# A fused AdaLN block on one core: value rows of two key groups projected token by feature, with the convolution's shift done by a DMA

## What is computed

```
h = layernorm(x) * (1 + ca) + sa                  # modulation rows from silu(c) @ wmod
qkv = h @ W_pack                                  # 16 query heads, 8 key and value groups, 128 wide
q, k = rope(q), rope(k)
k = conv_k[0] * k[token - 1] + conv_k[1] * k      # per group; token -1 counts as zero
v = conv_v[0] * v[token - 1] + conv_v[1] * v
attn = softmax(mask(q k^T / sqrt(128))) v         # causal, window of 128 tokens
x = x + ga * (attn @ W_o)
h = layernorm(x) * (1 + cb) + sb
x = x + gb * moe(h)                               # 32 experts, top 4, capacity 128, and a shared expert
```

## Time and profile before

| | |
|---|---|
| median of 3 runs | 765.53 us (765.27 to 766.3) |
| profiled execution | 769.37 us, of it 766.9 span from first to last instruction |
| mean granted TensorE clock | 0.99 of full speed |
| busy share of the span | PE 95%, PEld 81%, DVE 69%, ACT 61%, POOL 55% |
| chain that ended last | PE 76%, DVE 11%, ACT 6%, DMA 2% |
| share of that chain on the projections (L1335 into PJ) | 22% |

### The profile page before, as it was taken

One profiled execution on the slowest core, in us unless ns is written; L12 is line 12 of the kernel. 1 busy time (PEld: TensorE's weight loads), 2 busy tenths in 40 slices (PEclk: granted clock), 3 DMA queues, 4 the chain that ended last, 5 costly groups with the idle time before them and its releaser, 6 DMA issues.

```text
span 766.9 us, 12813 instructions
## 1 busy us (share of the span) xinstructions
PE 731.1 (95%) x4114; PEld 620.8 (81%) x4114; DVE 531.6 (69%) x1552; ACT 467.7 (61%) x1277; POOL 425.5 (55%) x337
## 2 busy tenths in 40 slices
PE   3899999999999999999999999999988999999997
PEld 3688889998899898889989888989866767777775
DVE  4598788679877768987776797778665215564373
ACT  5688878777886677788667777877554212222110
POOL 0644445554466488646647875654534517468356
PEclk9999999999999999999999999999999999999999
DMA  8960005800005011100401101040359689996772
GB/s 294 322 136 1 2 1 175 287 1 2 1 1 168 26 40 48 40 1 1 158 8 40 46 28 62 16 165 1 123 145 237 191 289 272 282 240 74 163 233 82
DMA packets 62353, 84.42 MB, mean 110 GB/s; under 512 B 6312, under 2 KB 50229, under 8 KB 62288
## 3 DMA queue, kind: packets, MB, share of 16 engines
q1 hardware_dynamic: 51440, 70.56, 29.8%
q0 software_dynamic: 7680, 8.95, 6.2%
q10 hardware_dynamic: 3168, 4.11, 1.5%
HBM read 54.81 MB, written 33.51 MB: 115 GB/s over the span
## 4 chain that ended last, share of the span: by engine, by line
PE 76%; DVE 11%; ACT 6%; DMA 2%; issue 2%; POOL 1%; SPq 0%; ACTq 0%; POOLq 0%
PE PJ L1335 22%; PE OUT L1443 9%; PE U L1428 6%; PE U L1388 6%; PE U L1593 5%; PE U L1417 4%; PE U L1387 3%; PE U L1429 3%; PE U L1335 3%; PE OUT L1539 3%; PE U L1539 2%; PE XB L1612 2%; PE OUT L1612 2%; PE XB L1335 2%; ACT U L546 1%
## 5 line engine op out<-in xcount | busy, mean ns | idle before, releaser
L768 POOL TENSOR_TENSOR qsw<-qsw,sinT 128x512 f32<-128x512 f32 x96 | 126.2, 1314 | 184.6 <-ACT qsw L533 183.7
L977 DVE CUSTOM_DVE_ANT_0 U<-U,mask 128x128 f32<-128x128 f32 (+1 forms) x256 | 86.6, 379 | 54.8 <-PE U L1388 54.4
L546 ACT ACTIVATE U<-U,nmax 128x128 f32<-128x128 f32 (+1 forms) x256 | 100.4, 392 | 32.2 <-DVE nmax L977 31.7
L1335 PE MATMUL PJ<-hT_hi,w_hi 128*128 128x512 f32 x256 | 113.8, 445 | 4.0 <-DVE hT_lo L951 3.7
L1335 PE MATMUL PJ<-hT_lo,w_hi 128*128 128x512 f32 x256 | 103.5, 404 | 0.0
L1335 PE MATMUL PJ<-hT_hi,w_lo 128*128 128x512 f32 x256 | 103.1, 403 | 0.0
L772 POOL TENSOR_TENSOR qr<-qr,qsw 128x512 f32<-128x512 f32 x64 | 82.5, 1289 | 31.3 <-DVE qr L965 30.8
L532 ACT ACTIVATE qsw<-PJ 64x512 f32<-64x512 f32 x96 | 57.0, 594 | 58.1 <-PE PJ L1335 49.3
L779 POOL DMA_INDIRECT slot_rows<-xn,sidx x64 | 64.4, 1006 | 45.6 <-issue 12.0
L1443 PE MATMUL OUT<-wo_hi,oT_hi 128*128 128x256 f32 x256 | 83.0, 324 | 1.4 <-DVE wo_lo L1001 1.2
L994 DVE TENSOR_TENSOR oT_lo<-U,oT_hi 128x256 fp32r<-128x256 f32 x128 | 54.1, 423 | 41.2 <-ACT oT_hi L553 41.0
(11 more groups left out here) (212 smaller groups left out, 1827.6 us busy)
## 6 DMA issues: line engine op xcount, KB each, us to landing
wgu<-in_dram SPq DMA_DIRECT2D x32, 352.0 KB, 9.4
expert_sum<-blank SPq DMA_DIRECT2D x3, 2176.0 KB, 17.8
slot_rows<-blank SPq DMA_DIRECT2D x1, 4624.0 KB, 26.3
late_sums<-expert_sum SPq DMA_DIRECT2D x9, 512.0 KB, 8.9
wd_a<-in_dram SPq DMA_DIRECT2D x12, 352.0 KB
wraw<-in_dram SPq DMA_DIRECT2D x8, 512.0 KB, 11.5
bcm<-mod_rows SPq DMA_DIRECT2D x8, 512.0 KB, 6.8
xe<-slot_rows ACTq DMA_DIRECT2D x10, 289.0 KB, 6.3
```

The lines of the kernel that those rows point to most:

```text
L546: last = act.activation(U[n % 3][:, a:z], U[n % 3][:, a:z], ACT.Exp, scale=-1.0, bias=nmax[:, n % 4, j:j + 1], accum_out=rsum[:, n % 4, j: ...
L768: pool.tensor_tensor(pair3(qsw[:, n % NQSW, :]), pair3(qsw[:, n % NQSW, :]), both(sinT[:, :]), ALU.mult).then_inc(t2_done, 1)
L977: last = dve.tensor_tensor_reduce(out=U[n % 3][:, a:z], in0=U[n % 3][:, a:z], in1=allowed, scale=-float(HD) ** -0.5, scalar=3.4e38, op0=AL ...
L1335: last = pe.matmul(out_ap, a(c), b_(c), start=(n == 0), stop=(n == len(steps) - 1))
```

## The change

The values are projected the other way round: the tokens of `hT` are the weights and 256 columns of `w_pack`, two value groups, are the moving side. One value turn makes one sequence of two groups, two blocks of 128 tokens by 256 features in one bank, with 12 matmuls of 256 columns. There are still 32 value turns, listed with the others in `TURNS`: each group of four units has one (group 0 has two, the last none), so the turns run one ahead and LEAD becomes 5. The order in which the projection weights are prepared (`W_ORDER`) changes with it.

The tokens now lie on partitions, and the shift by a token is a shift by a partition. ACT scales the bank by the first tap, one activation per group, into a `qsw` slot (which value turns now share with q and k; slots go by turn number). `next_token` on ACT then issues two DMAs, from SBUF to SBUF: rows 0 to 126 of both blocks to partitions 1 to 127 of `vsh`, and the last row of block 0 to partition 0 of block 1. DVE multiplies the bank by the second tap into `vN`, and POOL adds `vsh` (`earlier_token`, one step after the evacuation, behind the rope of that step). `v_transpose`, `v_rows`, `vT` and `v0` are gone. A `qsw` slot is reused three turns later, after the rope of that turn, or after the DMAs if it was a value turn. `XB` is ordered by the hooks' own semaphores, and `yg` shares memory with `xnT_lo`, with one more wait in `post_gate`.

```diff
-LEAD = 4
-W_ORDER = (4, 0, 6, 1, 5, 2, 7, 3)
+LEAD = 5
+W_ORDER = (4, 0, 6, 1, 7, 5, 2, 3)
+TURNS = []
+for _G in range(NU // 4):
+    TURNS += [("k", _G, 0), ("q", _G, 0)]
+    TURNS += [("v", v, 0) for v in ((0, 1) if _G == 0 else (_G + 1,)) if v < NV]
+    TURNS += [("q", _G, 1)]
...
 @block.scalar
+            def project(u):
+                kind, i, _ = TURNS[u]
+                bank, slot = PJ[u % 2], u % NQSW
+                act.wait_ge(pj_ps, u + 1)
+                if u >= NQSW:
+                    if TURNS[u - NQSW][0] == "v":
+                        v = TURNS[u - NQSW][1]
+                        act.wait_ge(ld_vsh[v % 2], 32 * (v // 2 + 1))
+                    else:
+                        act.wait_ge(rope_done, rope_number(u - NQSW) + 1)
+                if kind == "v":
+                    for g in range(2):
...
+                        last = act.activation(qsw[:, slot, :].rearrange("p (t c) -> p t c", t=2)[:, :, heads],
+                                              bank[:, :].rearrange("p (t c) -> p t c", t=2)[:, :, heads], ACT.Copy,
+                                              scale=cwv[:, tap:tap + 1])
+                    last.then_inc(pj_act, 1)
                     return
...
+            def next_token(u):
+                v = TURNS[u][1]
+                rows_v = qsw[:, u % NQSW, :].rearrange("p (t c) -> p t c", t=2)
+                act.wait_ge(pj_act, u + 1)
+                if v >= 2:
+                    act.wait_ge(v_done, v - 1)
+                act.dma_start(vsh[1:PN, v % 2, :, :], rows_v[0:PN - 1, :, :]).then_inc(ld_vsh[v % 2], 16)
+                act.dma_start(vsh[0:1, v % 2, 1, :], rows_v[PN - 1:PN, 0, :]).then_inc(ld_vsh[v % 2], 16)
...
             for n in STEPS:
-                if 0 <= n - 1 < NU and n % 4 == 1:
-                    v_rows(n // 4)
-                if 0 <= n + 3 < NU:
-                    project(n + 3)
+                if 0 <= n + LEAD - 1 < NU:
+                    project(n + LEAD - 1)
                 if 0 <= n - 2 < NU:
                     head_high(n - 2)
+                if 0 <= n + LEAD - 1 < NU and TURNS[n + LEAD - 1][0] == "v":
+                    next_token(n + LEAD - 1)
                 if 0 <= n < NU:
                     exps_of(n)
...
 @block.gpsimd
+            def earlier_token(u):
+                if TURNS[u][0] != "v":
+                    return
+                v = TURNS[u][1]
+                pool.wait_ge(ld_vsh[v % 2], 32 * (v // 2 + 1))
+                pool.wait_ge(pj_dve, u + 1)
+                pool.tensor_tensor(v_tile(v), v_tile(v), vsh[:, v % 2, :, :], ALU.add).then_inc(v_done, 1)
...
             for n in STEPS:
-                if 0 <= n + 3 < NU:
-                    rope(n + 3)
+                if 0 <= n + LEAD - 1 < NU:
+                    rope(n + LEAD - 1)
+                if 0 <= n + LEAD - 2 < NU:
+                    earlier_token(n + LEAD - 2)
...
 @block.vector
+                    dve.tensor_tensor(v_tile(i).rearrange("p t (g d) -> p t g d", g=2),
+                                      PJ[u % 2][:, :].rearrange("p (t g d) -> p t g d", t=2, g=2), tap,
+                                      ALU.mult).then_inc(pj_dve, 1)
...
 @block.tensor
+                if kind == "v":
+                    for t in range(2):
+                        tk = slice(i % 2 * S + t * PN, i % 2 * S + (t + 1) * PN)
+                        last = halves(PJ[u % 2][:, t * 2 * HD:(t + 1) * 2 * HD], HC,
+                                      ((lambda c: hT_hi[:, p % 2, c, tk], lambda c: hT_lo[:, p % 2, c, tk]), weights))
...
-            def v_transpose(G):
...
-                    if n % 4 == 0:
-                        v_transpose(n // 4)
```

More of the change, by code:

```diff
@@ L251, in adaln_block @@
             sem(n) for n in ("var1", "rstd1_done", "xhat_done", "ht_ps", "ht_used", "h_hi_done", "h_lo_done"))
-        pj_ps, pj_act, pj_dve, t2_done, rope_done, k0_done, kc_done, vt_ps, vn_done = (
-            sem(n) for n in ("pj_ps", "pj_act", "pj_dve", "t2_done", "rope_done", "k0_done", "kc_done", "vt_ps", "vn_done"))
+        pj_ps, pj_act, pj_dve, t2_done, rope_done, k0_done, kc_done, v_done = (
+            sem(n) for n in ("pj_ps", "pj_act", "pj_dve", "t2_done", "rope_done", "k0_done", "kc_done", "v_done"))
         sc_ps, sneg_done, exp_done, rinv_done, norm_done, pt_ps, pt_done, pv_ps, ot_done = (
@@ L298, in adaln_block, with columns, w_chunks @@
         WO_PART = NH // len(WO_STEPS)
[L300 to L305, removed]
+        def columns(u):
+            kind, i, h = TURNS[u]
+            g = i % GROUPS
+            first = {"k": (NH + g) * HD, "q": (2 * g + h) * HD, "v": (NH + NKV) * HD + (g // 2) * 2 * HD}[kind]
+            j, at = divmod(first, WC)
+            return j, slice(at, at + (2 * HD if kind == "v" else HD))
+        def w_chunks(u):
+            return W_ORDER.index(columns(u)[0]) + 1
         def x_pair(p):
@@ L317, in pair3, with rope_number, rope_buffer, v_tile @@
             return ap.rearrange("p (b s) -> p b s", b=2)
[L319 to L324, removed]
+        def rope_number(u):
+            return sum(kind != "v" for kind, _, _ in TURNS[:u])
+        def rope_buffer(u):
+            kind, G, h = TURNS[u]
+            return kr[:, :] if kind == "k" else qr[:, h, G % 2, :]
+        def v_tile(v):
+            return vN[:, v // 2 % 2, v % 2, :, :]
         def later(n):
@@ L527, in project @@
                     return
-                rope = rope_number(m)
-                if rope >= NQSW:
-                    act.wait_ge(rope_done, rope - NQSW + 1)
                 half = HD // 2
-                act.activation(qsw[0:half, rope % NQSW, :], bank[half:HD, :], ACT.Copy)
-                act.activation(qsw[half:HD, rope % NQSW, :], bank[0:half, :], ACT.Copy).then_inc(pj_act, 1)
+                act.activation(qsw[0:half, slot, :], bank[half:HD, :], ACT.Copy)
+                act.activation(qsw[half:HD, slot, :], bank[0:half, :], ACT.Copy).then_inc(pj_act, 1)
@@ L1202, in _ @@
                     head_low(n - 2)
-                if n % 4 == 3 and n + 1 < NU:
+                if n % 4 == 3 and 0 <= n + 1 < NU:
                     k_conv((n + 1) // 4)
-                if 0 <= n + 3 < NU:
-                    project(n + 3)
+                if 0 <= n + LEAD - 1 < NU:
+                    project(n + LEAD - 1)
                 if 0 <= n < NU:
@@ L1422, in weighted_v @@
                 pe.wait_ge(pt_done, n + 1)
-                if n % 4 == 0:
-                    pe.wait_ge(vn_done, G + 1)
+                if G % 2 == 0 and n % 4 < 2:
+                    pe.wait_ge(v_done, G + b + 1)
                 o = U[n % 3][:, 0:S]
-                v = vN[:, G % 2, b * S:(b + 1) * S]
-                pe.matmul(o, v[:, 0:PN], pT[:, n % 2, 0:S], start=True, stop=False)
-                pe.matmul(o[:, PN:S], v[:, PN:S], pT[:, n % 2, S:S + PN], start=False, stop=True).then_inc(pv_ps, 1)
+                v = vN[:, G // 2 % 2, b, :, G % 2 * HD:(G % 2 + 1) * HD]
+                pe.matmul(o, v[:, 0, :], pT[:, n % 2, 0:S], start=True, stop=False)
+                pe.matmul(o[:, PN:S], v[:, 1, :], pT[:, n % 2, S:S + PN], start=False, stop=True).then_inc(pv_ps, 1)
             def output(n):
```

139 lines of the change are left out of this document (59 added, 80 removed).

## The result

The changed kernel takes 954.99 us (median of 4 runs, 949.93 to 956.37) beside 765.4 us (762.47 to 766.3) for the kernel before: 1.2465 times as long, 95% interval 1.2427 to 1.2504. The forecast was 855 us with a range of 798 to 945: the direction came out and the mechanism in part, the size did not, and the time lies outside the range. The profiled execution took 956.4 us with a span of 954.5, against 769.4 and 766.9 before: +187.6 us of span.

What follows compares the result with a forecast made beforehand. TensorE bounds the kernel before; the one-engine copy's loop was to replace it. Loop groups and extras +69 us, start +21, prologue and tail -1, together +89 on 765.5: 855 us, range 798 to 945.

Steps and rivals of the forecast that it cites:

- The loop: Per group: issue, landing, addition, k's rotation, k tap, value evacuation, next issue, 17.8 us, replacing TensorE as bound.
- the landing: The 127-row copy to vsh, on one DMA engine, lands after 11.9 us; bounds 10.7 to 12.6.
- the sum: Loop groups with extras +69 us, start +21, prologue and tail -1: +89 on the 765.5 us median, 855 us.
- landings under traffic: Copies landing late: 10 us beside the zeroing of the sums; 4 us for the pairs' own loads.
- scatters behind the addition, ACT's hooks, routing: Extras above the loop: scatters before k's rotation 7 us, hooks before value evacuation 7, three pair-routing groups 7.
- the start: First two copies, issued near 26 and 29 us under traffic, land near 45 and 56; +21 us.
- the tail: One projection fewer at the end, 1.48 us partly hidden; together with the longer prologue -1 us.
- the issues: ACT's two DMA issues take some 0.7 us while oT_hi is copied; exponentials behind wait for DVE's k convolution anyway.
- The cheap parts: Value projection +0.03 us a group, 1 us in all; ACT about even; POOL's addition 1.29 us a group.
- the first rival: Copy spread over the engines lands in 2.5 us, TensorE stays the bound: about -5, 760.5 us; chance 0.11.
- The third, "halfway": One engine slower alone, near 1070 us; halfway, landing 14.5, loop 20.4, +180, 945 us; chance of slower than 945: 0.05.
- the signs named for the forecast: Addition waits 5 to 6 us; score matmuls 17 to 19 apart, waiting for q's rotation or kc; TensorE about 85%.

Runs made afterwards that it cites:

- e8: The changed kernel with a separate qsw slot for values and POOL's addition one iteration later, behind the next k's rotation; 918.8 us.
- e2: The changed kernel with its two DMAs swapped, the single row issued first and the 127-row copy behind it; 938.5 us.
- e4: The changed kernel with the 127-row copy cut into 79 rows (one engine) and 48 rows (16 engines), plus the single row; 821.4 us.
- e6: The changed kernel without the shift's DMA copies and without POOL's addition; 751.0 us, 0.9835 of the kernel before.
- e7: The changed kernel without the shift's DMA copies but with POOL's addition (of zeros) kept in place; 763.1 us, 0.9989 of the kernel before.
- e1: The changed kernel with the 127-row copy cut into 112 and 15 rows, plus the single row; 787.2 us, 1.0256 times the kernel before.
- e12: e1's copies, addition behind the next k's rotation, issues behind the exponentials, then SyncE's in a new program order from the fourth value turn; 763.3 us.

## Why the forecast had the right direction and the wrong size

**The loop was a right step, but not the only bound.** A group of the kernel after without scatters or bulk traffic (a quiet one), in which the single row's issue passed in 0.56 us (timeline, POOL and ACT; idle time and releaser in brackets):

```profile
462.12 0.63 ACTq L563 DMA_DIRECT2D vsh<-qsw  x1
462.79 0.56 ACTq L564 DMA_DIRECT2D vsh<-qsw  x1
...
475.74 1.28 POOL L806 TENSOR_TENSOR vN<-vN,vsh 128x512 f32<-128x512 f32 x1 [6.03 <-DMA vsh<-qsw]
476.97 1.27 POOL L793 TENSOR_TENSOR qsw<-qsw,sinT 128x512 f32<-128x512 f32 x1
478.32 1.27 POOL L797 TENSOR_TENSOR kr<-kr,qsw 128x512 f32<-128x512 f32 x1
...
479.68 0.72 ACT L571 ACTIVATE k<-kr,cwk 128x512 f32<-128x512 f32 x1 [1.14 <-POOL kr L797]
...
480.79 0.83 ACT L547 ACTIVATE qsw<-PJ,cwv 128x256 f32<-128x256 f32 x2
...
481.65 0.66 ACTq L563 DMA_DIRECT2D vsh<-qsw  x1
```

Issue to addition 13.62, then addition, rotation, k tap, value evacuation, next issue: 19.53 us. The forecast's loop was 17.8 with a landing of 11.9; with 13.62 in its place it is 19.52, and the two other quiet groups in which the issue passed have 19.51 and 19.52. Behind the landing stand 5.91 us here and 5.9 in the forecast.

Twelve more quiet groups have the same landing, 13.6 to 13.7 us, but an issue of 4.1 to 4.4; from issue to issue they take 19.1 to 23.0 us, 21.0 in the mean. The chain through one of them, the next one after the group above (start, us, what), and a window of it (length, busy us of the five engines, granted clock, DMA share, GB/s):

```profile
482.34 4.38 ACTq L564
...
488.11 1.22 PE U L1452 x2
...
489.76 1.28 PE OUT L1467 x6
...
499.00 0.71 PE OUT L1467 x6
```

```profile
485.70:492.50 6.80, 4.39 (x16) 4.02 (x17) 4.21 (x12) 4.68 (x14) 2.38 (x2) 0.50 0.07 25
```

The landing does not stand in it. What does is the blocked issue, the exponentials and pT behind it, and then TensorE from 488.1 us to the next issue at 502.9. TensorE had stood 3.15 us for pT, and its first 4.4 us are at a granted clock of 0.50: the six output matmuls take 1.28 us, and 0.71 at 499.0 us, where the clock is 1.00 (493.5 to 503 us). With the landing's loop open (e8) the same twelve turns still take 20.9 us in the mean; with no issue blocked (e2) they take 19.8. So in these groups ACT's blocked issue was the longer bound and the landing's loop the one just below it; the loop sets the time where the issue passed and where the landing was late.

**The first term that failed: the landing.** 13.6 us, not 11.9 (12.0 with the wake-up, which the measured one holds), and beyond the upper bound of 12.6. Windows of the copy issued at 462.12 us:

```profile
463.00:464.00 1.00, 1.00 (x8) 0.91 (x7) 1.00 (x2) 0.61 (x3) 0.00 (x0) 1.00 0.04 8
464.00:465.00 1.00, 1.00 (x7) 0.83 (x6) 0.79 (x3) 1.00 (x4) 0.00 (x0) 1.00 0.12 26
465.00:466.00 1.00, 1.00 (x9) 0.90 (x7) 1.00 (x5) 0.97 (x3) 0.00 (x0) 1.00 0.08 16
466.00:468.00 2.00, 2.00 (x15) 1.84 (x15) 1.35 (x6) 1.96 (x8) 1.09 (x1) 1.00 0.07 26
```

A DMA share of 0.06 to 0.07 is one engine of 16, and 26 GB/s is the rate that the forecast took from the earlier trace rows. But the engine gets there only some 4 us after the issue. No row moves in the first 1.3 us; the three windows from 463 us hold 4, 8 and 4 rows of the copy, 8 to 16 GB/s (what else flows there is the single row and two packets of the queue of instructions, q14). The forecast gave everything besides the bytes 1.9 us, by a transfer that was spread over 16 engines; here it is 3.2 (e4 and after, above), and 127 rows at 0.082 are 10.4 for 10.0. The loop of 19.52 is 1.72 us longer than that of the forecast, 1.62 of it the landing: 30 groups x 1.72 = 52 us, over half of the 98.6 us by which the span's +187.6 exceeds the +89 of the sum.

**The second: landings under traffic, and what else stands above the loop.** The 30 groups take 658.0 us; 30 x 19.52 are 585.6, so 72 us come on top, where the sum had 35. In 14 of the 30 turns the landing is longer than 13.7 us. The excess over 13.65 adds up to 48 us, and 40 of them are in six turns with 17.5 to 21.7 us. Two of these lie beside the zeroing of the sums (12.5 us, where I had put 10), three beside a pair's stores and loads (24, where I had put 4 for the loads), one beside the shared weights (4); the other 7.5 us are turns with scatters, for which I had nothing. That is 34 us of the miss. The other 24 of the 72 us meet 21 in the sum (scatters behind the addition, ACT's hooks, routing), but by luck: 18 of them stand in the twelve quiet groups with the blocked issue, 12 x 1.5, and in e2, where no issue is blocked, the same turns stand only 4 us above its loop of 19.45. Some 14 us are therefore the block, for which the sum had nothing. 37 us of the miss in all.

**The third: the start,** +28.9 for +21. Timeline of ACT's queue and POOL:

```profile
25.81 1.22 ACTq L563 DMA_DIRECT2D vsh<-qsw  x1
...
29.17 6.62 ACTq L563 DMA_DIRECT2D vsh<-qsw  x1
35.82 17.77 ACTq L564 DMA_DIRECT2D vsh<-qsw  x1
...
49.24 1.26 POOL L806 TENSOR_TENSOR vN<-vN,vsh 128x512 f32<-128x512 f32 x1 [21.68 <-DMA vsh<-qsw]
65.22 1.26 POOL L806 TENSOR_TENSOR vN<-vN,vsh 128x512 f32<-128x512 f32 x1 [7.64 <-DMA vsh<-qsw]
...
69.77 0.82 ACT L547 ACTIVATE qsw<-PJ,cwv 128x256 f32<-128x256 f32 x2
```

The issues fell at 25.8 and 29.2 us, as estimated (26 and 29); the additions came at 49 and 65, where the landings were forecast near 45 and 56, and the evacuation of group 1 at 69.8 for 61 (39.94 before). 8 us of the miss. That the copies share an engine packet by packet and take 1.6 times as long by it was an estimate that no run shows; the first took 23.4 us from issue to addition, beside 13.6 in a quiet group. The blocked issue does not make this: in e2 only one issue of the start is blocked, for 7.6 us, and unit 3 is no earlier (68.78).

52 + 37 + 8, and 1 at the tail, are 98 of the 98.6 us.

**A step that was wrong: the issues.** The two DMA issues were to take "some 0.7 us" while one copy runs, and the exponentials behind them were to wait for DVE "anyway". They take 0.64 and mostly 4.3 us, the exponentials wait for them 124 us in all, and TensorE behind them, part of the time at a clock of 0.50; 134 us of the chain that ended last are the blocked issue. Taking it away alone gives only 16 us (e2), because the landing's loop lies just below; e8 shows what it costs with that loop open, a group of 21.9 in place of 15.9.

**The cheap parts** were right (e6: 13 us where 14.1 - 1 was said), with one exception: the addition was to cost nothing beside TensorE (some 4 us in the first rival, landings of the start included), and cost about 12 (e7).

**The rivals.** The first, a spread copy at -5 us, would have been wrong had the condition held: e1, spread by a cut and so with three issues, is 22 us slower than before, because the issues and the addition eat the gain of the transposes; only with the issues on another queue does it come to about no change (e12). The third, "halfway" with a landing of 14.5, a loop of 20.4 and 945 us, is nearest to what happened in its number, a landing of 13.6 to 15.0 with six late ones beside it and 21.9 a group; I had stopped the range there, with 0.05 beyond. Its reason, an engine that is slower alone, did not come out but for the first rows: once it runs, the copy moves 26 GB/s. Nor do its numbers fit each other: the middle of 11.9 and 18.8 is 15.4, near 960 us by the same sum, and a loop of 20.4 gives near 937. Of the signs named for the forecast some came: 5.5 us of waiting for the addition in the mean, 82% of TensorE for about 85, unit 2 at 59.9. Two did not: the groups from score to score are 17.3 to 25.4 us for 17 to 19, and what TensorE waits for most is pT (72 us), not POOL's rotation of q (2.0) or kc (12.6), which already spoke for ACT's queue.

## To carry to other kernels

Count the partitions of a copy before its bytes: 127 rows on one engine land after 13.6 us, 112 rows on sixteen after 2.5, and a copy that is not a multiple of sixteen partitions can be cut into one that is and a rest, as e1 cuts 127 rows in 112 and 15, on 16 and 15 engines (787 us for 955). Give a transfer that sits in a loop a price from a transfer of its own shape or a wide range, with its lateness under the traffic of that stage as a term of its own. When the removal of a large wait moves little, look for a second bound of the same length (here ACT's own DMA issues) and remove both at once before you drop the theory; and count each issue on a compute engine's queue as that engine's work (here 1.9 us a group for three issues: 9 us of the kernel by their place in the order, up to 13 by their queue). Issue a long copy on one engine last: what stood behind it on the queue here took 4.3 us in the median.

## Of the hardware, not expected

- An issue held its engine's queue for microseconds: behind a one-engine copy of 127 rows the next issue on ACT took 4.3 us in the median and 17.8 at most, against 0.54 to 0.65 from the third turn on with the order reversed (e2). In every fourth turn (counted from 0: 0, 4, 12, 16, 20, 24, 28; 1.45 us in turn 8) it passed in 0.56 to 0.58 us with the same copy in front, and in e8 in the same turns; why was not found. Behind 79 rows on one engine (e4) it passed in 0.54 to 0.73 us in 29 of 32 turns.
- A copy of 127 rows on one engine moves 26 GB/s once it runs, but 8 to 16 GB/s in the first microseconds of its flow (463 to 466 us).
- In the start the granted clock was 0.50 in the windows from 36 to 62 us; TensorE had run no matmul since 32.2, and the clock was still 0.50 when it had work again, from 56.6 to 62. It was 0.50 again in the loop, in the blocked group shown from 485.7 to 492.5 us, after TensorE had come to a stand at 485.0 (it had work again at 488.1); over the span the mean was 0.906 for 0.990 before. The sum had no term for it. None of the steps of the landing's loop is TensorE's, but in the groups that the blocked issue bounds the clock of 0.50 is part of the price (1.28 us for the six output matmuls that take 0.71 at 1.00).
